# Feed-forward LayerNorm moved from six split steps to one block per tile, and a signal per half of the out-projection's add

## The reference, cut to what matters

```python
x = L0_attn_src                                   # (8, 2048, 1024) float32
x = x + attn(layernorm(x), Wq, bq, Wk, bk, Wv, bv, Wo, bo)
x = x + ffn(layernorm(x), W_fc, W_proj)

# attn: 8 heads of 128, softmax inside blocks of 64 tokens, then @ Wo + bo
# ffn:
h = square(relu(x @ W_fc.T))                      # (.., 4096)
y = h @ W_proj.T                                  # (.., 1024)
# five steps of: mem = 0.9*mem + y - (mem > 1); spike = (mem > 1)
# the output of ffn is the mean of the five spikes
```

## Time and profile before

| | us |
|---|---|
| median of the runs (lowest, highest) | 1128.71 (1128.01, 1129.41) |
| the profiled execution | 1130.49 |
| span of its slowest core, core 4 | 1128.7 |
| spans of the other cores | 1116.3 to 1126.0 |
| core 4: PE busy | 829.4 |
| core 4: DVE busy | 458.0 |
| core 4: ACT busy | 426.9 |
| core 4: POOL busy | 267.2 |

### The profile page before, as it was taken

How to read it: one execution, slowest core, us unless ns; L and a number is a source line. 1 busy time by engine, 2 the same in 40 slices (tenths; PEclk the granted TensorE clock), 3 DMA queues, 4 the chain that set the end, 5 groups by cost and what they waited for, 6 DMA issues and landing times.

```text
span 1128.7 us, 19208 instructions; the slowest of 8 cores (1116.3 to 1128.7 us)
## 1 busy us (share of the span) xinstructions
PE 829.4 (73%) x6624; PEld 604.8 (54%) x6624; DVE 458.0 (41%) x466; ACT 426.9 (38%) x1097; POOL 267.2 (24%) x128
## 2 busy tenths in 40 slices
PE   0197369845994399656998979899897988979600
PEld 0144234433443344332886868778686877858600
DVE  0103221233113320334017649284773928465282
ACT  3142522253225413322454545545454444534300
POOL 3000000011000100000005345062543606245185
PEclk9998569955995589658998989999899999989855
DMA  9995760077004820364778969698896969879300
GB/s 161 197 229 101 151 132 0 1 139 161 1 1 91 164 46 1 74 133 167 222 245 262 305 198 312 205 318 269 250 324 201 317 215 308 290 215 301 138 0 37
DMA packets 127291, 194.19 MB, mean 172 GB/s; under 512 B 42208, under 2 KB 44256, under 8 KB 127200
## 3 DMA queue, kind: packets, MB, share of 16 engines
q1 hardware_dynamic: 108144, 151.03, 44.4%
q0 software_dynamic: 14448, 33.56, 16.4%
q10 hardware_dynamic: 4608, 8.39, 2.0%
HBM read 192.95 MB, written 25.17 MB: 193 GB/s over the span
## 4 chain that ended last, share of the span: by engine, by line
PE 55%; DMA 20%; DVE 10%; ACT 5%; POOL 4%; issue 3%; SPq 1%; ACTq 0%; DVEq 0%; POOLq 0%
PE psC L835 15%; PE psA L870 8%; PE psB L870 7%; DMA w1slab<-w1scratch 7%; DMA w1scratch<-w2stage 6%; DMA w2scratch<-w2stage 4%; DMA bv_sb<-bv 3%; DVE mem_q L929 3%; PE psA L609 3%; PE psB L609 3%; PE psA L337 2%; PE psA L357 2%; PE psB L337 2%; PE psB L376 2%; PE psA L376 2%
## 5 line engine op out<-in xcount | busy, mean ns | idle before, releaser
L835 PE MATMUL psC<-xn2t_sb,w1slab 128*128 128x256 bf16 x2048 | 274.1, 279 | 21.6 <-ACT xn2t_sb L760 11.7
L835 PEld LDWEIGHTS psC<-xn2t_sb,w1slab 128*128 128x128 bf16 x2048 | 203.5, 100 | 53.1 <-issue 25.7
L847 ACT ACTIVATE h_bf<-psC 128x256 bf16<-128x256 f32 x256 | 97.9, 383 | 220.6 <-PE psC L835 220.5
L870 PE MATMUL psA<-h_bf,w2slab 128*128 128x256 bf16 x1024 | 155.2, 275 | 6.8 <-ACT h_bf L850 4.1
L870 PE MATMUL psB<-h_bf,w2slab 128*128 128x256 bf16 x1024 | 154.5, 274 | 0.0
L924 POOL TENSOR_TENSOR acc_q<-acc_q,spk_q 128x2048 bf16<-128x2048 bf16 x21 | 129.4, 6163 | 62.5 <-DVE spk_q L920 62.5
L929 DVE SCALAR_TENSOR_TENSOR mem_q<-mem_q,y_sb 128x2048 f32<-128x2048 f32 x21 | 125.1, 5958 | 2.2
L850 ACT ACTIVATE h_bf<-h_bf 128x256 bf16<-128x256 bf16 x256 | 106.6, 417 | 24.9 <-ACT h_bf L847 1.8
L870 PEld LDWEIGHTS psA<-h_bf,w2slab 128*128 128x128 bf16 x1024 | 99.2, 98 | 24.8 <-issue 12.7
L219 POOL DMA_DIRECT2D wtmp<-Wfc x32 | 17.3, 544 | 400.7 <-PE psD L501 363.5
L870 PEld LDWEIGHTS psB<-h_bf,w2slab 128*128 128x128 bf16 x1024 | 100.7, 98 | 12.2
(11 more groups left out here) (119 smaller groups left out, 1093.5 us busy)
## 6 DMA issues: line engine op xcount, KB each, us to landing
w2slab<-w2scratch SPq DMA_DIRECT2D x128, 512.0 KB, 6.6
w1slab<-w1scratch SPq DMA_DIRECT2D x128, 512.0 KB, 7.6
x_sb<-x SPq DMA_DIRECT2D x4, 2048.0 KB, 44.1
wtmp<-Wpr POOLq DMA_DIRECT2D x16, 512.0 KB, 7.0
wtmp<-Wfc POOLq DMA_DIRECT2D x32, 256.0 KB, 7.0
w2scratch<-w2stage SPq DMA_DIRECT2D x32, 256.0 KB, 4.1
w1scratch<-w2stage ACTq DMA_DIRECT2D x32, 256.0 KB, 5.1
out<-x_sb POOLq DMA_DIRECT2D x16, 512.0 KB, 9.1
```

Source lines behind the costliest of these rows:

```text
L835: op("pe", lambda E, fc=fc, c=c, hp=hp, s1b=s1b: E.matmul(hp, s1b[:, c * 128:(c + 1) * 128], xn2t_sb[:, c * 256:(c + 1) * 256], start=(c = ...
L847: op("se", lambda E, fc=fc, hp=hp: E.activation(h_bf[fc % 2][:], hp, ACT.Relu), inc="se")
L870: E.matmul(tgt[:, mc * 256:(mc + 1) * 256], slb[:, m * 128:(m + 1) * 128], h_bf[fp % 2][:], start=(fp == 0 and m % 2 == 0), stop=(fp == 31 ...
```

## The change

Two edits.

1. In the out-projection each half's add (L628) now counts up DVE's semaphore, where only the second did, and `relQ[0]` to `relQ[3]` hold the event of their own half.
2. `ln2_a`, `ln2_b` and `ln2_c` go. A tile of the next pass is done by one `ln2_tile`, tile 0 at `fc` = 24 and tile 1 at `fc` = 28. Both tiles use column 0 of the small tensors.

```diff
@@ out-projection
-                       ALU.mult, ALU.add), inc="ve" if half == 1 else None)
+                       ALU.mult, ALU.add), inc="ve")
+                E_x2h[(jg, half)] = n["ve"]
...
-        relQ[0] = relQ[1] = ("ve", E_x2[4 * p + 2])
-        relQ[2] = relQ[3] = ("ve", E_x2[4 * p + 3])
+        relQ[0] = ("ve", E_x2h[(4 * p + 2, 0)])
+        relQ[1] = ("ve", E_x2h[(4 * p + 2, 1)])
+        relQ[2] = ("ve", E_x2h[(4 * p + 3, 0)])
+        relQ[3] = ("ve", E_x2h[(4 * p + 3, 1)])
@@ LayerNorm of a tile: the three functions become one
-    def ln2_a(p, jj):
+    def ln2_tile(p, jj):
...
-        op("ve", lambda E, xs=xs, jj=jj: E.reduce_sum(
-            sums[:, jj:jj + 1], xs, AX.X), inc="ve")
-        E_ln2red[jj] = n["ve"]
+        op("ve", lambda E, xs=xs: E.reduce_sum(sums[:, 0:1], xs, AX.X),
+           inc="ve")
+        E_red = n["ve"]
         wait("se", "pe", E_xn2t_fill[jj])
         op("se", lambda E, xs=xs, jj=jj: E.activation(
-            xn2_bf[jj][:], xs, ACT.Square, accum_out=sqsums[:, jj:jj + 1]),
+            xn2_bf[jj][:], xs, ACT.Square, accum_out=sqsums[:, 0:1]),
             inc="se")
...
-    def ln2_b(p, jj):
-        wait("ve", "ve", E_ln2red[jj])
-        wait("ve", "se", E_ln2sq[jj])
+        wait("ve", "ve", E_red)
+        wait("ve", "se", E_sq2)
...
         E_veps2 = n["ve"]
         wait("se", "ve", E_veps2)
-        op("se", lambda E, jj=jj: E.activation(
-            vtmp[:, jj:jj + 1], veps[:, jj:jj + 1], ACT.Ln), inc="se")
+        op("se", lambda E: E.activation(vtmp[:, 0:1], veps[:, 0:1],
+                                        ACT.Ln), inc="se")
...
-    def ln2_c(p, jj):
...
-        wait("ve", "se", E_ln2rs[jj])
+        wait("ve", "se", E_rstd2)
@@ inside a pass
-                if p + 1 < PF and fc in (16, 18, 20, 22, 24, 26):
-                    part, jj2 = divmod((fc - 16) // 2, 2)
-                    [ln2_a, ln2_b, ln2_c][part](p + 1, jj2)
+                if p + 1 < PF and fc in (24, 28):
+                    ln2_tile(p + 1, (fc - 24) // 4)
```

More of the change, by code:

```diff
@@ L235, in build_nc @@
     E_x2 = {}
+    E_x2h = {}
     war = {"tta": 0, "p": 0}
@@ L685, in build_nc @@
     E_xn2t_fill = [0, 0]
-    E_ln2red = [0, 0]
-    E_ln2sq = [0, 0]
-    E_ln2rs = [0, 0]
-    def ln2_a(p, jj):
+    def ln2_tile(p, jj):
         jg = 2 * p + jj
@@ L695, in ln2_a @@
             wait("se", "ve", E_x2_all)
-        op("ve", lambda E, xs=xs, jj=jj: E.reduce_sum(
-            sums[:, jj:jj + 1], xs, AX.X), inc="ve")
-        E_ln2red[jj] = n["ve"]
+        op("ve", lambda E, xs=xs: E.reduce_sum(sums[:, 0:1], xs, AX.X),
+           inc="ve")
+        E_red = n["ve"]
         wait("se", "pe", E_xn2t_fill[jj])
         op("se", lambda E, xs=xs, jj=jj: E.activation(
-            xn2_bf[jj][:], xs, ACT.Square, accum_out=sqsums[:, jj:jj + 1]),
+            xn2_bf[jj][:], xs, ACT.Square, accum_out=sqsums[:, 0:1]),
             inc="se")
-        E_ln2sq[jj] = n["se"]
-    def ln2_b(p, jj):
-        wait("ve", "ve", E_ln2red[jj])
-        wait("ve", "se", E_ln2sq[jj])
+        E_sq2 = n["se"]
+        wait("ve", "ve", E_red)
+        wait("ve", "se", E_sq2)
         for b_ in [
-            lambda E, jj=jj: E.tensor_single_scalar(
-                nmean[:, jj:jj + 1], sums[:, jj:jj + 1], -1.0 / D, ALU.mult),
-            lambda E, jj=jj: E.tensor_single_scalar(
-                mmean[:, jj:jj + 1], sums[:, jj:jj + 1], 1.0 / D, ALU.mult),
-            lambda E, jj=jj: E.tensor_mul(
-                mmean[:, jj:jj + 1], mmean[:, jj:jj + 1], mmean[:, jj:jj + 1]),
-            lambda E, jj=jj: E.scalar_tensor_tensor(
-                veps[:, jj:jj + 1], sqsums[:, jj:jj + 1], 1.0 / D,
-                mmean[:, jj:jj + 1], ALU.mult, ALU.subtract),
-            lambda E, jj=jj: E.tensor_single_scalar(
-                veps[:, jj:jj + 1], veps[:, jj:jj + 1], EPS, ALU.add),
+            lambda E: E.tensor_single_scalar(
+                nmean[:, 0:1], sums[:, 0:1], -1.0 / D, ALU.mult),
+            lambda E: E.tensor_single_scalar(
+                mmean[:, 0:1], sums[:, 0:1], 1.0 / D, ALU.mult),
+            lambda E: E.tensor_mul(mmean[:, 0:1], mmean[:, 0:1],
+                                   mmean[:, 0:1]),
+            lambda E: E.scalar_tensor_tensor(
+                veps[:, 0:1], sqsums[:, 0:1], 1.0 / D, mmean[:, 0:1],
+                ALU.mult, ALU.subtract),
+            lambda E: E.tensor_single_scalar(
+                veps[:, 0:1], veps[:, 0:1], EPS, ALU.add),
         ]:
@@ L724, in ln2_b @@
         wait("se", "ve", E_veps2)
-        op("se", lambda E, jj=jj: E.activation(
-            vtmp[:, jj:jj + 1], veps[:, jj:jj + 1], ACT.Ln), inc="se")
+        op("se", lambda E: E.activation(vtmp[:, 0:1], veps[:, 0:1],
+                                        ACT.Ln), inc="se")
         wait("se", "se", n["se"])
-        op("se", lambda E, jj=jj: E.activation(
-            rstd[:, jj:jj + 1], vtmp[:, jj:jj + 1], ACT.Exp, scale=-0.5),
-            inc="se")
-        E_ln2rs[jj] = n["se"]
-    def ln2_c(p, jj):
-        jg = 2 * p + jj
-        xs = x_sb[:, jg * 1024:(jg + 1) * 1024]
-        wait("ve", "se", E_ln2rs[jj])
+        op("se", lambda E: E.activation(rstd[:, 0:1], vtmp[:, 0:1],
+                                        ACT.Exp, scale=-0.5), inc="se")
+        E_rstd2 = n["se"]
+        wait("ve", "se", E_rstd2)
         op("ve", lambda E, xs=xs, jj=jj: E.tensor_scalar(
-            xn2_bf[jj][:], xs, nmean[:, jj:jj + 1], rstd[:, jj:jj + 1],
+            xn2_bf[jj][:], xs, nmean[:, 0:1], rstd[:, 0:1],
             ALU.add, ALU.mult), inc="ve")
         E_norm2_d[(p, jj)] = n["ve"]
-    def ln2_tile(p, jj):
-        ln2_a(p, jj)
-        ln2_b(p, jj)
-        ln2_c(p, jj)
     def ln2_transposes(p, jj):
```

## The result

The changed kernel's median is 1149.44 us over 9 runs (1146.66 to 1202.64), against 1129.45 over 8 runs of the kernel before (1126.71 to 1248.64); the upper ends are disturbed runs, which the comparison leaves out. The ratio is 1.0177, with a 95% interval from 1.0159 to 1.0195, so 1.8% slower. Forecast: 1149.5 us. The profiled execution took 1148.1 us.

A forecast was written before the change was run, and what follows sets the result against it. PE was taken to set the pace, with ACT's order deciding whether its h is ready. 22.5 us of new stalls less 1.7 removed and 0 for the first edit gave +20.8 on 1128.71: 1149.5 us, range 1144 to 1156.

The forecast's parts named there:

- What bounds, and the slack: Feed-forward passes: PE sets the pace at 1.745 us per step and forgives 0.36 us of lateness of ACT's Relu.
- First edit, 0 us: Out-projection: the adds are done before the Q groups' wait, so the finer signal releases nothing, 0 us.
- The chain: At fc 24 and 28: Square to next Relu 2.93 us, 1.61 us of PE stall per tile, 14 tiles, 22.5 us.
- What is hidden: DVE runs both tiles' reduces ahead of their blocks; the product in mmean, 1.65 us before, should be short.
- What is removed, and which core counts: The stalls ln2_b makes at fc 20 go, about 1.7 us on core 4, taken as the core that counts.
- The sum: On core 4: 22.5 - 1.7 - 0 = +20.8 us, for a median of 1149.5 us, 1.8% slower.
- Rival 1: Behind the stalls TensorE's clock falls: 2.9 us per drop, 1164 us for five tiles, 1190 for 14; chance 0.07.
- Rival 2: At fc 24 DVE isn't free or mmean's product is slow: 1.5 us in six tiles, +9, 1158 us; chance 0.03.
- Rival 3: At pass starts, w1slab waits of 9.9 us shrink as loads spread; half of that gives 1144.5 us; chance 0.07.
- Rival 4: At fc 24 and 28 ACT hides the new chain, 0.1 us per tile, 1129 us, not slower; chance 0.03.

The follow-up runs named there:

- x1_signal: The kernel before with the first edit alone (signal per half of the out-projection's add); 1.0002 times before.
- x2_block: The kernel before with the second edit alone (LayerNorm blocks at fc 24 and 28); 1.0162 times before.
- x3_split_late: The kernel before, its LayerNorm split kept but four of six parts moved two chunks later, last normalize at fc 28; 0.9993 times before.
- x4_one_chunk: The changed kernel with one chunk's Relu and square between a tile's Square and the rest of its block; 0.9964 times before.
- x10_one_chunk_again: The same kernel as x4_one_chunk, measured again; 0.9976 times before.
- x5_reduce_in_line: The changed kernel with DVE's reduce waiting for ACT's Square in the 14 tiles inside the passes; 1.0433 times before.
- x6_three_ahead: The changed kernel with three of the five small DVE operations ahead of the wait for the Square; 1.0060 times before.
- x7_block_early: The changed kernel with its LayerNorm blocks at fc 16 and 20 instead of 24 and 28; 1.0573 times before.
- x7b_block_early: The same kernel as x7_block_early, measured again; 1.0594 times before.
- x8_product_ts: x7_block_early with the product in mmean written as a tensor_scalar with one tensor input; 1.0598 times before.
- x9_both_ts: x8_product_ts with veps, too, written as a tensor_scalar with one tensor input; 1.0502 times before.

## Why the prediction came out

**What bounds, and the slack.** Right. PE needs its h every 1.745 us and forgives a constant. Its size was read from two late starts as 0.36 us; by the table above it is 1.31 - (1.28 - 0.32) = 0.35.

**First edit, 0 us.** Right: 1.0002 alone.

**The chain.** Right: Square to DVE 1.24 (1.23 said), Square to Relu 2.94 (2.93 said), stall 1.63 (1.61 said). The second tile costs as much as the first: 798.19 is as late as the groups at fc 24 of most passes. The prediction treated all 14 as equal; three per core are 0.1 to 0.4 us worse, at the same places on every core. At fc 28 of the first pass ACT's square starts late behind its own Relu, as on core 4 after:

```profile
584.88 0.42 ACT L838 ACTIVATE h_bf<-h_bf 128x256 bf16<-128x256 bf16 x1 [0.37 <-ACT h_bf L835]
```

At fc 24 of the second pass the Relu comes 3.19 us behind the Square instead of 2.94, and in the fourth pass PE itself starts 0.1 to 0.15 us late. I know no cause for these. With them the stalls come to 11 x 1.63 + 2 x 1.90 + 1.7 = 23.4 us against 22.5.

**What is hidden.** Right: ACT's wait for `veps` is 1.40 us in all 14 tiles, so no reduce is ever in the way, and the product in `mmean` is short in all of them (0.16 us).

**What is removed, and which core counts.** The mechanism was right, the step "core 4 is the one that counts" was not. The stalls at fc 20 are gone on every core, but core 4 ends 14 us ahead of the slowest one now. Two things made it slow before: it came to its first psA group late (540.1 us, against 532.6 after), and it lost time in the starts of its passes, 15.5 us in the first six steps of all passes against 1.5 after. There PE waits for `w1slab`: 9.9 us before, while the list of waits of core 4 after has no such line, and core 1 has

```profile
PE psC L824 <- DMA w1slab<-w1scratch: 7.4, 9, 1.7
```

These waits move from core to core between executions, and so does the part ahead of the passes, which the prediction took as unchanged. Cores 4 and 5 show a pattern: before, core 4's first psA group of the feed-forward part started at 540.1 us and core 5's at 533.7; after, at 532.6 and 542.2. In both, the later one of the two loses more in the starts of its passes. It holds in 48 of the 52 pairs (0 and 1, 2 and 3, and so on) of the 13 profiled executions. Why is not shown. The forecast survived this because the added stalls are equal on all cores and the removed ones are small beside them: 1.2 us on core 3 to 6.0 on core 5, 3.4 on average, where the prediction took core 4's 1.7 for all.

**The sum.** +20.8 us said, 1149.44 - 1129.45 = 20.0 measured (18.0 to 22.0 by the interval). That it came so close is in part luck: 22.5 was 0.9 to 1.0 too low, since some stalls are longer, and 1.7 was 1.7 too low as a figure for all cores. The average over the cores is 23.5 - 3.4 = 20.1.

A sum that needs no choice of a core: the time from the psA group of chunk 13 to that of chunk 31, over all eight passes, as a mean of the eight cores of the profiled execution. It was 252.4 us before and 272.5 after. For all kernels, less the 252.4, beside the change in time that the ratios give:

| | chunks 13 to 31, us | time, us |
|---|---|---|
| x1_signal | -0.2 | 0.2 (-2.0 to 2.4) |
| x2_block | 20.3 | 18.3 (15.9 to 20.8) |
| after | 20.1 | 20.0 (18.0 to 22.0) |
| x3_split_late | -2.6 | -0.8 (-3.1 to 1.5) |
| x4_one_chunk | -3.0 | -4.1 (-5.8 to -2.3) |
| x10_one_chunk_again | -3.1 | -2.7 (-4.4 to -1.1) |
| x5_reduce_in_line | 49.5 | 48.9 (44.9 to 52.9) |
| x6_three_ahead | 9.0 | 6.8 (4.5 to 8.9) |
| x7_block_early | 68.2 | 64.7 (62.2 to 67.0) |
| x7b_block_early | 66.4 | 67.0 (65.1 to 69.0) |
| x8_product_ts | 66.4 | 67.5 (65.7 to 69.4) |
| x9_both_ts | 56.3 | 56.7 (54.2 to 59.0) |

The left column lies within the interval of the right one in ten of twelve; `x6_three_ahead` and `x7_block_early` are 2.2 and 3.5 us faster than it says. Each left number is one execution, so a difference of 2 us between them means little.

**Rival 1, the clock.** Didn't occur. The idles of 1.47 to 1.74 us are under the 2.04 that did no harm, as the prediction had it. `x5_reduce_in_line` shows its condition from the other side: at 2.85 to 3.12 us of idle the clock falls behind 4 to 8 of the 14 stalls of a core. The Trainium skill ("TensorE: Matmul & The Clock Gate", section on the second failure mode, depth-cycling) says that frequent short idles can swing the clock; with 14 of 1.5 us a core the trace doesn't agree, and with 14 of 3 us it does in part.

**Rival 2, DVE not free or the slow product along.** Didn't occur at fc 24. At fc 16 it does (`x7_block_early`), with a far larger price, since DVE is busy longer than the 1.5 us of the product. (The 1.5 was read from the longest of six products; the other five are held for 1.2 us.)

**Rival 3, the starts of the passes give some back.** Not by anything that can be told here: by the table above there is nothing left over for it in the changed kernel, and 2.2 and 3.5 us in two of the others, of which one, `x7_block_early`, shows none when it is measured again (67.0 against 66.4). The sums of the starts don't settle it. Over the first six steps of all passes and the eight cores, the time beyond 1.747 us a step is 74 us before, 75 in `x1_signal`, 74 in `x3_split_late`, 61 after, and 54, 49 and 37 in `x2_block`, `x6_three_ahead` and `x5_reduce_in_line`, which looks like a gain wherever a block stands. But it is one execution of each, with 1.5 to 19.5 us per core, and one kernel alone differs as much: 52 us in `x4_one_chunk` and 37 when it was measured again, 58 in `x7_block_early` and 79 when that was.

**Rival 4, ACT hides the chain.** Didn't occur. `x4_one_chunk` shows what it would have taken: one chunk's Relu and square between Square and Ln.

## What to carry to other kernels

An engine runs its instructions in order, so a round trip to another engine and back costs its full length to whatever is queued behind it, even if its own work is 0.4 us. Count the chain from the first instruction to the one that a third engine waits for, subtract the slack (read it from a place where something was already late), and multiply; here that gave 1.61 us for 1.63. Sum the stalls that go away over all cores, too, and not only on the one that happened to be the slowest of one execution. The cure is one piece of other work between the two halves of the round trip, not more: one chunk between them removed all of it, but for 0.17 us at one place of each core.

And a small operation on 128x1 isn't always small: where POOL streams through SBUF beside it, choose forms with one tensor input.
